# Own rows transposed into the bank of the edge sums in gcn_first and attend, a third row buffer in attend, and shorter lags in gcn_first

## The reference

```python
# gcn_layer: self loops are added once more, dinv = 1/sqrt(deg)
h = x @ W
msg = h[src] * (dinv[src] * dinv[dst])[:, None]
out = segment_sum(msg, dst) + b        # relu, then a second layer 256 -> 128
...
# attention layer
att = sigmoid(x[src] @ W_att[:d] + x[dst] @ W_att[d:] + b_att)
aggregated = segment_sum((x[src] @ W_msg + b_msg) * att, dst)
gi, gh = aggregated @ W_ih.T + b_ih, x @ W_hh.T + b_hh
r, z = sigmoid(i_r + h_r), sigmoid(i_z + h_z)
n = tanh(i_n + r * h_n)
h_new = (1 - z) * n + z * x            # then a batch norm over all nodes
```

## Time and profile before

| what | value |
|---|---|
| three runs | 5292.63 us median, 5287.95 to 5303.6 |
| the profiled execution | 5276.13 us, span 5274.4 us |
| TensorE, VectorE, ScalarE, GpSimd busy | 86%, 69%, 51%, 57% |
| mean granted TensorE clock | 0.932 |
| gcn_first | from 252 to 830 us of the span |
| attend | from about 3830 to 4520 us of the span |

### The profile page before, as it was taken

How to read it: one execution, slowest core, us unless ns; L and a number is a source line. 1 busy time by engine, 2 the same in 40 slices (tenths; PEclk the granted TensorE clock), 3 DMA queues, 4 the chain that set the end, 5 groups by cost and what they waited for, 6 DMA issues and landing times. The chain is left out here.

```text
span 5274.4 us, 102984 instructions
## 1 busy us (share of the span) xinstructions
PE 4554.6 (86%) x26356; PEld 3497.7 (66%) x26356; DVE 3618.0 (69%) x11417; ACT 2701.4 (51%) x6655; POOL 3012.1 (57%) x2949
## 2 busy tenths in 40 slices
PE   4499996666699989999999997888789999878777
PEld 4478885555466656676766765777656666777777
DVE  8568776666566645555555564788768888876776
ACT  2645555766444442222222222777777777664555
POOL 0077775777677755444444443777476666007776
PEclk5599998888799999999999998999999999999999
DMA  4889995666599985445455553788877777784554
GB/s 149 288 243 291 285 283 179 197 196 201 190 328 329 329 306 166 171 163 172 165 168 170 165 171 98 231 246 246 241 232 235 236 235 228 260 308 144 152 152 141
DMA packets 576022, 1145.98 MB, mean 217 GB/s; under 512 B 114083, under 2 KB 121034, under 8 KB 572810
## 3 DMA queue, kind: packets, MB, share of 16 engines
q1 hardware_dynamic: 475802, 924.73, 51.4%
q0 software_dynamic: 100080, 219.67, 16.3%
HBM read 705.95 MB, written 438.05 MB: 217 GB/s over the span
## 5 line engine op out<-in xcount | busy, mean ns | idle before, releaser
L881 POOL DMA_INDIRECT s_rows<-t_h,s_index x417 | 519.9, 1247 | 712.4 <-DVE s_index L874 613.4
L881 POOL DMA_INDIRECT g_rows<-t_x,g_index x417 | 418.1, 1003 | 372.0 <-DVE g_index L874 260.2
L881 POOL DMA_INDIRECT cb_rows<-t_x,cb_index x417 | 395.1, 947 | 381.9 <-DVE cb_index L874 257.0
L881 POOL DMA_INDIRECT at_rows<-t_m,at_index x417 | 445.8, 1069 | 260.4 <-DVE at_index L874 151.3
L881 POOL DMA_INDIRECT s_rows<-t_v,s_index x417 | 404.0, 969 | 203.8 <-issue 120.1
L881 POOL DMA_INDIRECT s_rows<-t_x,s_index x417 | 420.6, 1009 | 151.7 <-issue 121.9
L1805 ACT ACTIVATE s_hid<-bank,sb_c 128x512 f32<-128x512 f32 x196 | 124.1, 684 | 731.0 <-PE bank L1778 731.0
L881 POOL DMA_INDIRECT g_rows<-t_h,g_index x417 | 402.6, 965 | 161.1 <-issue 126.5
L947 PE MATMUL bank<-g_onehot,g_rows 128*128 128x168 f32 (+4 forms) x980 | 239.3, 406 | 200.7 <-DMA g_rows<-t_h,g_index 195.0
L1842 DVE TENSOR_TENSOR s_rout<-bank,s_x 128x512 f32<-128x512 f32 x98 | 67.8, 692 | 491.2 <-PE bank L1790 491.2
L947 PE MATMUL bank<-s_onehot,s_hi 128*128 128x168 f32 (+4 forms) x1470 | 350.8, 282 | 56.3 <-DVE s_lo L915 49.3
(11 more groups left out here) (356 smaller groups left out, 12688.1 us busy)
## 6 DMA issues: line engine op xcount, KB each, us to landing
s_scale<-inv_d SPq DMA_DIRECT2D x196, 256.0 KB
htt<-s_ht SPq DMA_DIRECT2D x98, 512.0 KB
t_h<-s_hout SPq DMA_DIRECT2D x98, 512.0 KB
s_ht<-htt SPq DMA_DIRECT2D x98, 512.0 KB
t_m<-s_mout SPq DMA_DIRECT2D x98, 264.0 KB
at_own<-t_m SPq DMA_DIRECT2D x98, 264.0 KB
t_x<-so_x SPq DMA_DIRECT2D x98, 256.0 KB, 4.3
g_own<-t_x SPq DMA_DIRECT2D x98, 256.0 KB
```

The costliest lines, as they stand in the source:

```text
L881: pool.indirect_dma_start(out=self.rows[:, self.row(q, k), :], out_offset=None, in_=self.table[0:NPAD, :], in_offset=bass.IndirectOffsetOn ...
```

## The change

- The two scaled identities `id_own1` and `id_own` go, and the own rows are turned by four TensorE transposes against `ident`, which open the bank (start at the first, no stop); the edge sums follow and accumulate onto them.
- The factor that was in the identity moves to ScalarE: in gcn_first `raise_own` multiplies the loaded own rows by own1 in place, and `sums` waits for it (`raised`) in place of the load; in attend a second small activation in `weigh` multiplies the four attention columns by `own`.
- gcn_first: down goes from lag 5 to 3, up from 3 to 2, relu from 4 to 2, scale from 6 to 3, rest from 7 to 4, scale_sums from 2 to 0; loads of x and both stores move two steps closer; ScalarE's order becomes scale, take_hi, raise_own, relu, and VectorE's prepare_split, rest, scale_sums.
- attend: three `hn` buffers, so `move` waits for the store four groups back, and not at all where the group is kept.

```diff
--- before.py
+++ after.py
@@ -223,7 +223,6 @@
 
     idx = sb("idx", [P, SLOTS], U32)
     dcol = sb("dcol", [P, SLOTS])
-    dsg = sb("dsg", [P, SLOTS])
     dinv_n = sb("dinv_n", [P, T * BLK])
     dinv2_n = sb("dinv2_n", [P, T * BLK])
     inv_n = sb("inv_n", [P, T * BLK])
@@ -233,8 +232,6 @@
     own = sb("own", [P, 1])
     general = sb("general", [P, 1], I32)
     own1 = sb("own1", [P, 1])
-    id_own1 = sb("id_own1", [P, P])
-    id_own = sb("id_own", [P, P])
     bn_acc = sb("bn_acc", [P, T + BLK - 1, 6])
     bn_mv = sb("bn_mv", [P, 2])
     ln_eps = sb("ln_eps", [P, 1])
@@ -810,8 +807,6 @@
                 dve.tensor_copy(general[:, :], total[:, 0:1])
                 then(dve.tensor_scalar(own[:, :], total[:, 0:1], -1.0, 1.0, ALU.mult, ALU.add))
                 then(dve.tensor_scalar(own1[:, :], own[:, :], 1.0, None, ALU.add))
-                dve.tensor_scalar(id_own1[:, :], ident[:, :], own1[:, 0:1], None, ALU.mult)
-                dve.tensor_scalar(id_own[:, :], ident[:, :], own[:, 0:1], None, ALU.mult)
                 then(dve.reciprocal(by_group(inv_n), deg[:, :, :]))
                 dve.tensor_scalar(selfinv_n[:, :], inv_n[:, :], own[:, 0:1], None, ALU.mult)
                 invert_roots(len(PIECES) - 1)
@@ -935,7 +930,7 @@
             self.arrived(pe, q)
             pe.wait_ge(self.ready, q.t + 1)
 
-        def sum_by_feature(self, pe, q, banks, close=True):
+        def sum_by_feature(self, pe, q, banks, open_=True, close=True):
 
             todo = pieces(q.r)
             for h, to in enumerate(banks):
@@ -945,7 +940,8 @@
                         sources = [(self.hi, self.row(q, k)), (self.lo, self.row(q, k))]
                     for s, (part, at) in enumerate(sources):
                         last = pe.matmul(to[:, a:b], part[:, at, h * P:(h + 1) * P],
-                                         self.onehot[:, self.place(q, k), off:off + b - a], start=(i + s == 0),
+                                         self.onehot[:, self.place(q, k), off:off + b - a],
+                                         start=(open_ and i + s == 0),
                                          stop=(close and i + 1 == len(todo) and s + 1 == len(sources)),
                                          skip_group_check=True)
             return last
@@ -1094,6 +1090,12 @@
     def planes(tile):
 
         return tile[:, :].rearrange("f (b p) -> f b p", b=BLK)
+
+    def turn_into(pe, to, rows):
+
+        for b in range(BLK):
+            pe.matmul(nodes(to)[:, b, :], rows(b), ident[:, :], start=(b == 0), stop=False, is_transpose=True,
+                      skip_group_check=True)
 
     def row_of(a, t):
         return a[bass.ds(t, 1), :].broadcast_to([P, GRP])
@@ -1411,7 +1413,7 @@
             hout, rout = ph.pair("hout", [P, GRP]), ph.pair("rout", [P, GRP])
             loaded, loaded_x, loaded_s = ph.sems("loaded"), ph.sems("loaded_x"), ph.sems("loaded_s")
             agged, relued, scaled, rested = ph.sem("agged"), ph.sem("relued"), ph.sem("scaled"), ph.sem("rested")
-            hidden, lowered, link = ph.sem("hidden"), ph.sem("lowered"), ph.sem("link")
+            hidden, lowered, link, raised = ph.sem("hidden"), ph.sem("lowered"), ph.sem("link"), ph.sem("raised")
             st_h, st_r = ph.sems("stored_h"), ph.sems("stored_r")
             block = ctx.enter_context(nc.Block())
 
@@ -1426,24 +1428,20 @@
                 over_groups(sp, [
                     (0, lambda q: load(sp, q, own_rows[q.u][:, :], own_group(t_x0, q.t), loaded[q.u], e.summed)),
                     (1, lambda q: load(sp, q, scale_row[q.u][:, :], row_of(dinv_d, q.t), loaded_s[q.u], agged)),
-                    (6, lambda q: load_x(sp, q, xin, loaded_x, rested)),
-                    (7, lambda q: store(sp, q, group_of(t_h0[0:NPAD, :], q.t), hout[q.u][:, :], scaled, st_h)),
-                    (8, lambda q: store(sp, q, group_of(r1, q.t), rout[q.u][:, :], rested, st_r))])
+                    (4, lambda q: load_x(sp, q, xin, loaded_x, rested)),
+                    (5, lambda q: store(sp, q, group_of(t_h0[0:NPAD, :], q.t), hout[q.u][:, :], scaled, st_h)),
+                    (6, lambda q: store(sp, q, group_of(r1, q.t), rout[q.u][:, :], rested, st_r))])
                 all_stored(sp, st_h, st_r)
 
             @block.tensor
             def _(pe):
                 def sums(q):
                     e.fetched(pe, q)
-                    pe.wait_ge(loaded[q.u], q.n * 16 + 16)
+                    pe.wait_ge(raised, q.t + 1)
                     if not is_first(q.t):
                         pe.wait_ge(agged, q.t - 1)
-                    e.sum_by_feature(pe, q, [bank[q.u]], close=False)
-                    for b in range(BLK):
-                        last = pe.matmul(nodes(bank[q.u])[:, b, :], own_rows[q.u][:, b * D:(b + 1) * D],
-                                         id_own1[:, :], start=False, stop=(b == BLK - 1),
-                                         skip_group_check=True)
-                    last.then_inc(e.summed, 1)
+                    turn_into(pe, bank[q.u], lambda b: own_rows[q.u][:, b * D:(b + 1) * D])
+                    e.sum_by_feature(pe, q, [bank[q.u]], open_=False).then_inc(e.summed, 1)
 
                 def up(q):
                     pe.wait_ge(agged, q.t + 1)
@@ -1465,7 +1463,7 @@
                                              start=(h == 0), stop=(h == 1), skip_group_check=True)
                     last.then_inc(lowered, 1)
 
-                over_groups(pe, [(1, sums), (5, down), (3, up)])
+                over_groups(pe, [(1, sums), (3, down), (2, up)])
 
             @block.scalar
             def _(act):
@@ -1489,7 +1487,12 @@
                                               scale=col(dinv_n, q.t * BLK + b))
                     last.then_inc(scaled, 1)
 
-                over_groups(act, [(4, relu), (6, scale), (0, lambda q: e.take_hi(act, q))])
+                def raise_own(q):
+                    act.wait_ge(loaded[q.u], q.n * 16 + 16)
+                    act.activation(own_rows[q.u][:, :], own_rows[q.u][:, :], ACT.Copy, scale=own1[:, 0:1])\
+                       .then_inc(raised, 1)
+
+                over_groups(act, [(3, scale), (0, lambda q: e.take_hi(act, q)), (0, raise_own), (2, relu)])
 
             @block.vector
             def _(dve):
@@ -1517,7 +1520,7 @@
                                       b2_r[:, :, :].rearrange("p b f -> p (b f)"), ALU.add)\
                        .then_inc(rested, 1)
 
-                e.on_vector(dve, [(2, scale_sums), (0, lambda q: e.prepare_split(dve, q)), (7, rest)])
+                e.on_vector(dve, [(0, lambda q: e.prepare_split(dve, q)), (4, rest), (0, scale_sums)])
 
 
     def gcn_second():
@@ -2014,16 +2017,16 @@
             mine = ph.pair("mine", [P, BLK, D])
             agg = ph.pair("agg", [P, GRP])
             r, zg, mix, ng = (ph.pair(n, [P, GRP]) for n in ("r", "z", "mix", "n"))
-            hn = ph.pair("hn", [P, GRP])
+            hn = ph.pair("hn", [P, GRP], n=KEEP - 1)
             loaded_x, loaded_m = ph.sems("loaded_x", XS), ph.sems("loaded_m")
-            opens, weighed = ph.sem("opens"), ph.sem("weighed")
+            opens, weighed, kept_own = ph.sem("opens"), ph.sem("weighed"), ph.sem("kept_own")
             gated, mailed, agged = ph.sem("gated"), ph.sem("mailed"), ph.sem("agged")
             crossed, opened, mixed, tanhed = ph.sem("crossed"), ph.sem("opened"), ph.sem("mixed"), ph.sem("tanhed")
             hx, loaded_h = ph.pair("hx", [P, GRP], n=4), ph.sems("loaded_h", 4)
             joined = ph.sem("joined")
             GATES = ((3, 4), (2, 7))
             link, link3, moved = ph.sem("link"), ph.sem("link3"), ph.sem("moved")
-            stored = ph.sems("stored")
+            stored = ph.sems("stored", KEEP)
             block = ctx.enter_context(nc.Block())
 
             def width_of(q, k):
@@ -2032,7 +2035,7 @@
                 return wide(k)
 
             def new_h(q):
-                return kept_slab(kept, q) if q.d % KEEP == 0 else hn[q.u][:, :]
+                return kept_slab(kept, q) if q.r == 0 else hn[q.r - 1][:, :]
 
             @block.gpsimd
             def _(pool):
@@ -2070,12 +2073,8 @@
                     pe.wait_ge(mailed, q.t + 1)
                     if not is_first(q.t):
                         pe.wait_ge(agged, q.t - 1)
-                    e.sum_by_feature(pe, q, [bank[q.u]], close=False)
-                    for b in range(BLK):
-                        last = pe.matmul(nodes(bank[q.u])[:, b, :], mine[q.u][:, b, :],
-                                         id_own[:, :], start=False, stop=(b == BLK - 1),
-                                         skip_group_check=True)
-                    last.then_inc(e.summed, 1)
+                    turn_into(pe, bank[q.u], lambda b: mine[q.u][:, b, :])
+                    e.sum_by_feature(pe, q, [bank[q.u]], open_=False).then_inc(e.summed, 1)
 
                 def gates(q):
                     pe.wait_ge(agged, q.t + 1)
@@ -2120,6 +2119,8 @@
```

(6 more changed lines are left out.)

## The result

The changed kernel takes 5329.26 us in the median of five runs (5325.2 to 5334.51); the kernel before, in five runs, 5291.67 (5283.87 to 5303.6). The ratio is 1.0074, 95% interval 1.0062 to 1.0087: slower by 0.7%, 37.6 us between the medians. The forecast was 5344 us, range 5285 to 5408, slower. The profiled execution of the changed kernel has a span of 5327.5 us, 53.1 more than that of before.

The account below looks back on a forecast made before the run. It took TensorE to bound gcn_first and attend before the change, and rings of waits between engines after; +73 (gcn_first ring) - 7 (drain) + 11 (clock) - 26 (attend) = +51 us, 5344 us, range 5285 to 5408.

Parts of the forecast that it names:

- The ring in gcn_first: In gcn_first, the cycle down, scale, take_hi, lo, sums, down sets the period at 6.33 us against 5.57: +73 us.
- the step from lo to TensorE: In gcn_first's ring, the hop from lo's end to the first weight load of the waiting sums: 0.22 us.
- The step back to ScalarE: In gcn_first's ring, the hop from TensorE's end of down to ScalarE's start of scale: 0.04 us.
- The clock: In gcn_first, TensorE 80% busy gets a granted clock of 0.97, as in combine: +11 us.
- The rival of a further fall: In gcn_first, the clock falls to gcn_second's 0.83, costing 70 us in place of 11: 5403 us, chance 0.05.
- The end of the phase: In gcn_first's drain, down's lag is two shorter, saving two steps of 3.5 us: -7 us.
- raise_own off the path: In gcn_first, the ScalarE copy of about 0.66 us is ready no later than lo, adding nothing to the path.
- attend: In attend, the ring gate, blend, tanh, open, weigh, gate becomes the bound at 6.60 us against 6.865: -26 us.
- the second small activation: In attend's ring, the added activation delays the next instruction by 0.23 us, bounds 0.19 and 0.3.
- The third buffer: In attend, it allows the gain: VectorE's waits for stores (22.3 + 21.2 us and more) would otherwise lie in the ring.
- The sum: Whole kernel: +73 - 7 + 11 - 26 = +51 us, 5344 us against the median.
- The faster rival, open ring: The ring in gcn_first does not bind; its period falls to between 5.55 and 5.40 us: 5250 us, chance 0.12.

Follow-up runs that it names:

- (1): Changed kernel with take_hi and raise_own ahead of scale in gcn_first's ScalarE order; 5269.07 us, ratio to the kernel before 0.9966.
- (2): Changed kernel with gcn_first's scale at lag 4 in place of 3, ahead of take_hi as before; gcn_first 573.6 us, period 5.61 us.
- run 4: Kernel before with only the new lags and orders of gcn_first, own rows by matmul, no raise_own; 5405 us, gcn_first period 6.87 us.
- (7): run 3's kernel loading only 16 of 512 scale-row columns from the third group on; gcn_first period 5.56 us.
- run 3: Changed kernel with gcn_first's lags and orders as before, raise_own last on ScalarE; gcn_first 573.4 us, period 5.56 us.
- 8: Changed kernel with gcn_first's scale at lag 4 and attend's own factor as the sigmoid's bias; 5254.59 us, ratio to the kernel before 0.9932.
- 9: run 3's kernel with rest's last VectorE instruction adding zero with one operand instead of b2; gcn_first period 5.549 us.
- (6): Changed kernel with attend's two row buffers and store wait as before; attend 729.2 us, period 7.13 us.
- (5): Changed kernel with attend's second small activation replaced by a bias of the sigmoid; 5316.91 us, ratio to the kernel before 1.0054.

## Why the prediction was right, point by point

- **The ring in gcn_first**: right, and shown: opened by order (1) or by distance (2) it is gone, and with the matmuls in it (4) it is longer. By term, in the turn shown: scale to take_hi 1.01 for 1.00, take_hi to lo 0.68 for 0.70, lo 0.69, down with its first load 2.06 for 2.06, sums 1.51 for 1.57, from TensorE to ScalarE 0.14 for 0.04. Together 6.15 for 6.28 us, and with the larger groups 6.26 for 6.33. The term that was mis-sized is the step from lo to TensorE: 0.06 for 0.22. I took it from one step whose sums begin with edge matmuls; in run 4, where they do too, it is 0.22 or more in 49 turns of 78 and 0.05 in the rest. The step back to ScalarE was too short in the sum, 0.04 for a mean of 0.18, and took most of that back.
- **The clock**, +11 us forecast: it stayed at 1.00 in gcn_first with TensorE busy 388.77 of 460 us. combine's 0.97 at 78% was a poor neighbour; the term was 0. The rival of a further fall did not come. In the runs with the ring open, with the same four transposes a group, the clock of the stretch is 0.97 (7) to 1.00 (3, 8, 9). The Trainium skill (TensorE: Matmul & The Clock Gate, Part 4: PE-mode transpose) states that transposes do not engage the full clock; the 1.00 of this stretch shows no such loss where they stand among matmuls, and in none of these runs was it under 0.97 there.
- **The end of the phase**, -7 us: from the last own load to the next phase it is 31.1 us for 35.7, so -4.6.
- gcn_first in all: +56 for +77 us. Of the 21 us, 11 are the clock and 13 the periods, less 2 at the end of the phase. The 13 are 0.07 us of the ring (7 us) and, for the rest, that I reckoned from steady stretches: from first to last group the period was 5.60 before, where I took 5.57, and 6.22 after, where the steady stretch has 6.26.
- **raise_own off the path**: right, it ended 0.11 us or more ahead of lo in all 80 turns; and run 4, without it, has the same loss.
- **attend**: the mechanism was right (gate, blend, tanh, open, weigh, gate; waits for stores gone; VectorE waits for the gates in 74 of 87 steps), the size was not: -5.7 us for -26. The mis-sized term is the second small activation: 0.33 us from start to start, where I took 0.23 from the one beside it and gave 0.3 as its bound. That makes the ring 6.70 on average instead of 6.60; undisturbed it turns in 6.74, as two of four steps take 0.04 and 0.11 us more than the 6.59 that I had for each, and the last 0.03 us of the period (6.77) are single steps in which something else was late. And against the 6.865 us of the steady stretch the phase as a whole had run at 6.83 before.
- **The third buffer**: right that the change rests on it: 36 us (6).
- **The sum**: +51 us forecast; +53.1 between the two profiled executions, but +38 between the medians (5329 us for a forecast of 5344), the profiled execution before having been 15.5 us under its median. That the sum came so close is partly luck: gcn_first was put 21 us too high and attend's gain 20 us too high.
- The faster rival, open ring, was put at 5250 us; runs 1 to 3, with the ring open, show what it misjudged: a gather did not get cheaper (0.998 us in run 3, not 0.966), so the period stayed at 5.56 to 5.63 us. Only if every gather took the 0.94 us of an unstretched one would GpSimd come to 4.25 x (0.94 + 0.305) = 5.3 us, an estimate.

## What to carry to other kernels

When lags between engines are shortened, write down for each stage which earlier stage stands ahead of it in its own engine's order and what that one waits for: a cycle that returns to the same stage one group later sets a floor for the period, and it can be far over any engine's work. Moving one unrelated stage behind the critical one, or one step further away, opens it: here by one edited line, with 56 to 61 us back. And an instruction added on an engine with idle time is free only if no such cycle runs through that engine's order: in attend TensorE's work fell by 0.45 us a group, 44 us in all, but with 0.33 us more on a ScalarE that had been busy three quarters of the time the phase gained 6; taking most of that out again (5) gave 20 more.

## What the runs showed of the hardware

- A ScalarE activation of 4 columns took 0.19 us with no column operand and 0.28 to 0.30 with a scale or bias read from a column; from start to start 0.23 against 0.31 to 0.33.
- After a wait for VectorE, TensorE's first weight load came 0.05 us after lo's end in 70 of 80 turns of the changed kernel, where a transpose comes first, and 0.13 in 10; in run 4, where an edge matmul comes first, it came after 0.22 to 0.25 us in 49 of 78 and after 0.05 in 29. Why was not tried.
- Four float32 transposes with strided output into PSUM took 0.39 us from their first weight load to the next one's in all 80 turns of the changed kernel's gcn_first, where combine's have 0.44; with the edge matmuls that accumulate onto them sums took 1.51 us where 1.57 had been added up.
- Gathers issued from GpSimd took 0.94 us each; of those that began during a VectorE instruction with two SBUF operands 54 of 156 took 1.05 to 1.6 us in run 3, of the other 182 two did. With the DMA share at 0.80 in place of 0.93 their mean was the same.
